# A sixth state pair on GpSimd, a later gated sum and earlier probabilities in a fused Perceiver kernel

## The chip, the cores and the metric

The kernel runs on one core of one Trainium2 chip. The metric is the device time of one execution in microseconds (us). Five engines work side by side, each through its own list of instructions in order: TensorE (PE), VectorE (DVE), ScalarE (ACT), GpSimd (POOL) and SyncE, which starts the DMAs. They meet only through semaphores: an instruction raises one when it is done, and another engine waits until it has a certain value.

## The reference, cut to what matters

The reference is a Perceiver block on x (128 x 32 tokens of 256 numbers) with a context of 128 x 257 tokens. Six layers follow each other, each adding to x. The kernel computes them in two loops; the change is in the first, which holds three things:

```python
x = x + _L0_xattn_ref(ctx_1024, _layernorm(x), wq, wk, wv)      # softmax attention on the context
x = x + _L0_attn_ref(_layernorm(x), W_in, b_in, W_gate, ...)    # gated selective scan, 16 states
# of _L1_xattn_ref, which is linear attention on the same context, only its key side:
k = relu(ctx @ Wk + bk) + eps; k = k / softplus(scale)
k = k**3 / norm(k**3) * norm(k);  kv = k.T @ v;  ks = k.sum()

def _selective_scan(x, delta, A_log, B_mat, C_mat, D_vec):      # inside _L0_attn_ref
    A = -jnp.exp(A_log); c0 = C_mat[0]
    def step(h, inp):
        x_t, d_t = inp
        h = h * jnp.exp(A * d_t[..., None]) + (x_t * d_t)[..., None] * B_mat
        return (h, h @ c0)
    ...
    return y + x * D_vec
```

The 16 states of a channel don't mix: each is a scan of its own over time, and y is a weighted sum of the 16 results. The result is `gate * (y + x * D) @ W_out.T + b_out`.

## The kernel before, in words

**Tiling.** The 128 sequences are cut into 32 groups of four (128 rows of tokens), and four groups make a chunk. The 512 inner channels of the scan are four blocks of 128 channels; one block of one chunk (a 128 x 512 tile) is one scan job, so there are 32 jobs.

**Steps.** The first loop has 37 steps, G = 0 to 36, and software-pipelines four stages (`stages(G)`): A, group G: attention and the first three and a half parts of its keys; C, group G-1: the end of its keys, its Gram products with the context, its key sums; J, scan job G-4; Z, the end of scan job G-5. Steps 5 to 31 have all four stages. Every fourth step from G = 8 on (g == 0) also has the output projection of an earlier chunk ("output step"), and every step with g == 3 up to G = 27 the query projection of the next chunk ("query step"); the others are called plain.

**A scan job.** TensorE projects hT to `delta`, `x` and `gate`, all three through one PSUM bank, so each must be drained before the next is made. ScalarE drains delta (L769), x to `dx` (L787) and gate with a tanh (L811). VectorE makes `u` = x * delta in PSUM (L991). Then for each of eight pairs q of states: ScalarE makes two decays exp(-A delta) into `abuf[q % 2]` (`act_decay`, L696); VectorE runs two scans (`dve_scan`, L943). A buffer of decays is free again when the scan that read it is done, so decay q waits for scan q-2. The results of a pair are added up in one of two ways. Pairs 0, 6 and 7 (BY_PE) go to `gL`, and TensorE multiplies them with diagonal matrices into the bank `ps_y` (`pe_states`, L570). Pairs 1 to 5 (BY_POOL) are weighted in place by ScalarE (`act_weigh`, L705) and added up in `yac` by GpSimd (`pool_add`, L868 for pair 1 with dx, L871 for the others). At the end VectorE makes the gated sum: ps_y + yac[0], + yac[1], times (1 + gate), three instructions (L1010, L1012, L1014) into `yg`, which the output projection reads.

**Keys and attention.** For each of the four sequences b of a group TensorE makes keys (`pe_keys`, L509 and L512), VectorE drains them (`dve_keys`, L952), ScalarE squares them (L718), GpSimd cubes them (`pool_cube`, L861), ScalarE sums the squares of the cubes (L725), GpSimd makes the ratio of norms for two sequences (`pool_ratio`, L851 and L855), ScalarE normalises (L736), TensorE makes the Gram product (`pe_gram`, L524) and ScalarE drains it (L744). The attention: scores (L500), maximum (L969, L974), probabilities (L780), their transposes (L627, L628), a copy (L1001), the product with the context (L643), `o_sb` (L1020), its transposes (L654), the copy `oT` (L1029), the projection (L666), and the layer norm (L834).

**Order.** Nothing is planned at run time. The order on each engine is what `pe_step`, `act_step`, `pool_step` and `dve_step` write down by hand for a step; the semaphores only hold an instruction back.

## Time and profile before

| | us |
|---|---|
| median of 3 executions | 2247.94 (2247.15 to 2249.84) |
| the profiled execution | 2246.96 |
| its span, first to last instruction | 2245.1 |
| busy: TensorE / VectorE / ScalarE / GpSimd | 1864.1 / 1592.2 / 1475.6 / 1207.8 |
| granted TensorE clock, mean | 0.917 |

The page gives these. The 40 slices of the page show TensorE at 80 to 90% busy until about 1290 us of the span and a dip around 1350 to 1450 us, where the first loop runs out (its last scan jobs have no keys beside them) and the second begins. Two more kinds of view are used below: the instructions of one engine in order of time (start, duration, what it is, and in brackets how long the engine had been idle before it and who released it), and the busy time of all engines between two given times.

### The profile page before, as it was taken

Reading aid. Unit: us, or ns where it says so; the run is one execution under the profiler, and the core shown is the slowest. Engines: PE = TensorE matmul, PEld = TensorE weight load, DVE = VectorE, ACT = ScalarE, POOL = GpSimd, SP = SyncE. Lnnn points to the kernel's source line nnn. Section 1 sums busy time; section 2 is a strip of 40 time slices with the busy share of each in tenths; the row PEclk is TensorE's granted clock in tenths of the full one; section 3 lists DMA queues with packets and bytes.
Section 4 is the critical chain, followed back from the end, with each engine's and each line's share of the span. In section 5 each row is a group of like instructions: output and inputs, shape, how many; then the busy total and the mean of one; then the engine's idle time right before and its main releaser. Section 6 shows DMA issues by size and latency. Waiting matters only on the chain. (4 is left out here: it accounts for less than half of the span.)

```text
span 2245.1 us, 41621 instructions
## 1 busy us (share of the span) xinstructions
PE 1864.1 (83%) x14355; PEld 1256.0 (56%) x14355; DVE 1592.2 (71%) x2945; ACT 1475.6 (66%) x3431; POOL 1207.8 (54%) x1300
## 2 busy tenths in 40 slices
PE   4898988988988898899899774378989898888964
PEld 2655555555555555555555432356666666676743
DVE  3348777767867867867858787457788878878763
ACT  2558877777868868867868776124666666656654
POOL 1435555545546545545545633156777767767751
PEclk8999999999999999999999997678889999989876
DMA  7321112112211211111111110100000000000000
GB/s 187 111 90 60 62 55 67 60 54 67 66 56 59 78 59 62 60 61 60 59 52 60 38 47 5 54 7 9 13 12 12 12 12 12 12 12 12 10 8 10
DMA packets 48370, 103.20 MB, mean 46 GB/s; under 512 B 6384, under 2 KB 25072, under 8 KB 43376
## 3 DMA queue, kind: packets, MB, share of 16 engines
q1 hardware_dynamic: 48240, 101.57, 14.4%
q8 instruction: 69, 1.13, 0.2%
q14 instruction: 61, 0.50, 0.1%
HBM read 93.03 MB, written 8.52 MB: 45 GB/s over the span
## 5 line engine op out<-in xcount | busy, mean ns | idle before, releaser
L861 POOL TENSOR_TENSOR kcube<-kcube,ksq 128x512 f32<-128x512 f32 x128 | 178.0, 1391 | 487.2 <-ACT ksq L718 487.2
L696 ACT ACTIVATE abuf<-delta,cols 128x496 f32<-128x496 f32 x512 | 337.6, 699 | 30.5 <-DVE gP L943 19.0
L871 POOL TENSOR_TENSOR yac<-yac,gP 128x1024 f32<-128x1024 f32 x128 | 301.7, 2357 | 11.4 <-ACT gP L705 10.3
L943 DVE TENSOR_TENSOR_SCAN gP<-abuf,ps_s 128x512 f32<-128x512 f32 x256 | 293.3, 1196 | 0.6 <-POOL yac L871 0.6
L943 DVE TENSOR_TENSOR_SCAN gL<-abuf,ps_s 128x512 f32<-128x512 f32 x192 | 223.2, 1206 | 57.7 <-ACT abuf L696 57.6
L583 PE MATMUL ps_kv<-hT,w_pT 128*128 128x512 f32 x384 | 194.0, 630 | 75.0 <-ACT delta L769 72.5
L512 PE MATMUL ps_kv<-w_k,cT 128*128 128x256 f32 x1024 | 256.1, 393 | 0.0
L524 PE MATMUL ps_kv<-kcube,cx 128*128 128x256 f32 x1024 | 246.8, 385 | 9.4 <-ACT kcube L736 8.6
L524 PEld LDWEIGHTS ps_kv<-kcube,cx 128*128 128x128 f32 x1024 | 192.7, 192 | 62.5 <-ACT kcube L736 20.3
L512 PEld LDWEIGHTS ps_kv<-w_k,cT 128*128 128x128 f32 x1024 | 184.7, 190 | 49.4 <-issue 29.4
L570 PE MATMUL ps_t<-gL,diag 128*128 128x512 f32 x384 | 184.7, 605 | 15.4 <-DVE gL L943 13.1
L705 ACT ACTIVATE gP<-gP,cols 128x512 f32<-128x512 f32 x256 | 169.1, 709 | 0.0
L583 PEld LDWEIGHTS ps_kv<-hT,w_pT 128*128 128x128 f32 x384 | 72.8, 198 | 158.9 <-ACT delta L769 99.7
L851 POOL TENSOR_TENSOR rat<-s,roots 128x8 f32<-128x8 f32 x64 | 105.8, 1654 | 79.6 <-ACT junk L725 79.6
L952 DVE TENSOR_TENSOR kcube<-ps_kv,epi 128x512 f32<-128x512 f32 x128 | 86.5, 676 | 80.1 <-PE ps_kv L512 80.1
L725 ACT ACTIVATE junk<-kcube 128x256 bf16<-128x256 f32 x256 | 103.3, 406 | 52.0 <-POOL kcube L861 52.0
L736 ACT ACTIVATE kcube<-kcube,rk 128x256 f32<-128x256 f32 x256 | 108.6, 495 | 28.3 <-POOL rk L855 28.3
L570 PEld LDWEIGHTS ps_t<-gL,diag 128*128 128x128 f32 x384 | 71.5, 193 | 91.5 <-issue 68.8
L1462 PE MATMUL ps_t<-pjT,gT 128*128 128x256 f32 x512 | 117.5, 383 | 0.0
L1591 POOL TENSOR_TENSOR kTm<-kTe,mask 128x1024 f32<-128x1024 f32 x32 | 92.4, 2888 | 45.9 <-ACT kTe L1501 45.9
L744 ACT ACTIVATE Gs<-ps_kv 128x512 f32<-128x512 f32 x128 | 74.5, 582 | 63.1 <-PE ps_kv L524 62.9
L718 ACT ACTIVATE ksq<-kcube 128x256 f32<-128x256 f32 x256 | 102.9, 405 | 8.4 <-DVE kcube L952 8.4
(312 smaller groups left out, 4279.8 us busy)
## 6 DMA issues: line engine op xcount, KB each, us to landing
cT<-in_h_ctxT SPq DMA_DIRECT2D x32, 1028.0 KB, 4.9
cx<-in_ctx SPq DMA_DIRECT2D x32, 1024.0 KB, 5.3
xT<-in_h_xT SPq DMA_DIRECT2D x8, 512.0 KB, 3.9
xcur<-in_x SPq DMA_DIRECT2D x32, 128.0 KB, 2.0
x_mid<-xb SPq DMA_DIRECT2D x16, 256.0 KB, 2.2
x_c<-x_mid SPq DMA_DIRECT2D x32, 128.0 KB, 2.0
out<-y SPq DMA_DIRECT2D x32, 128.0 KB, 1.7
kv_all<-vleft SPq DMA_DIRECT2D x8, 256.0 KB, 11.1
```

The source lines that it names most:

```text
L512: last = pe.matmul(bank[:, j * D:(j + 1) * D], cT[G % 2][:, b, dc, j * P:(j + 1) * P], w_k[:, dc, :], start=False, stop=(dc == DC - 1), sk ...
L524: last = pe.matmul(ps_g[:, dc * D:(dc + 1) * D], cx[G % 2][:, b, j, dc * P:(dc + 1) * P], kcube[N % RING][:, j, :], start=(j == 0), stop=( ...
L570: last = pe.matmul(ps_y[:, :], diag[:, J % CB, 2 * k + i, :], pe_home(J, q)[:, i, :], start=(k == 0 and i == 0), stop=(k == NPE - 1 and i ...
L583: last = pe.matmul(ps_p, w_pT[:, dc, r * P:(r + 1) * P], hT[s % 2][:, dc, :], start=(dc == 0), stop=(dc == DC - 1))
L696: act.activation(abuf[q % 2][:, i, :].rearrange("p (b t) -> p b t", t=T)[:, :, 1:T], delta[J % 2][:, :].rearrange("p (b t) -> p b t", t=T) ...
L705: last = act.activation(t[:, i, :], t[:, i, :], ACT.Copy, scale=w_st[:, J % CB, 2 * q + i:2 * q + i + 1])
L736: last = act.activation(t[:, j, :], t[:, j, :], ACT.Copy, scale=rk[k % 2][:, 2 * i + j:2 * i + j + 1])
L851: pool.tensor_tensor(rat[p][:, :], s26[p][:, :], roots[:, :], ALU.pow).then_inc(S["rat_ready"], 1)
L861: pool.tensor_tensor(t[:, :, :], t[:, :, :], ksq[:, :, :], ALU.mult).then_inc(S["k3_ready"], 1)
L871: pool.tensor_tensor(yac[:, :, :], yac[:, :, :], pool_home(q)[:, :, :], ALU.add).then_inc(S["pacc_done"], 1)
L943: dve.tensor_tensor_scan(dst[:, i, :], abuf[q % 2][:, i, :], ps_u[:, :], 0.0, ALU.mult, ALU.add).then_inc(S["scan_done"], 1)
L1462: last = pe.matmul(ps_c1[:, 0:D], gT[:, f, :], W["pjT"][:, f, :], start=(f == 0), stop=(f == FC - 1))
```

## The change: what it does

Pair 6 goes from the TensorE way to the ScalarE and GpSimd way: ScalarE weights it (behind decay 0 of the next job) and GpSimd adds it. TensorE keeps pairs 0 and 7; the state product of pair 0 is issued a step later, between the delta and the x projection. `gate` and `yac` get two buffers each. On VectorE the gated sum moves from ahead of `o_sb` to behind `oT`, ahead of scan 2, and the key-sum addition (L1082) from behind to ahead of scan 5. On ScalarE the probabilities move from behind weighing 5, a Gram drain and the normalising to right behind delta. On GpSimd the additions move ahead by one place: 4 ahead of the ratio, 5 ahead of cube 0, 6 ahead of cube 1, 2 ahead of the rstd1 power, 3 ahead of cube 3. The diff, with one line of context:

```diff
NPAIR = NST // 2
-BY_POOL = (1, 2, 3, 4, 5)
+BY_POOL = (1, 2, 3, 4, 5, 6)
 BY_PE = tuple(q for q in range(NPAIR) if q not in BY_POOL)
...
         dx = sb("dx", [P, TS])
-        gate = sb("gate", [P, TS])
+        gate = [sb(f"gate{i}", [P, TS]) for i in range(2)]
         abuf = [sb(f"abuf{i}", [P, 2, TS]) for i in range(2)]
...
         gP = [sb(f"gP{i}", [P, 2, TS]) for i in range(3)]
-        yac = sb("yac", [P, 2, TS])
+        yac = [sb(f"yac{i}", [P, 2, TS]) for i in range(2)]
         yg = sb("yg", [P, CB, TS])
...
 
+        if Z is not None:
+            pe_states(pe, Z, 0)
         if J is not None:
             pe_project(pe, "x", J)
-        if Z is not None:
-            pe_states(pe, Z, 6)
         if C is not None:
...
             pe_finish(pe, C)
-        if J is not None:
-            pe_states(pe, J, 0)
         if g == 0 and sc >= 2:
...
 
-    def pool_home(q):
+    def pool_home(J, q):
         k = BY_POOL.index(q)
-        return yac if k == 0 else gP[(k - 1) % 3]
+        return yac[J % 2] if k == 0 else gP[(k - 1) % 3]
 
...
 
-        t = pool_home(q)
+        t = pool_home(J, q)
         for i in range(2):
...
             act.activation(delta[J % 2][:, :], ps_p, ACT.Relu, bias=b_dl[:, J % CB:J % CB + 1]).then_inc(S["pj_act"], 1)
+        if A is not None:
+            act.wait_ge(S["negm_ready"], A + 1)
+            if A:
+                act.wait_ge(S["pT_full"], A)
+            act.activation(pr[:, :], ps_s[:, 0:L], ACT.Exp, bias=negm[:, 0:1], scale=rstd0[:, 0:1],
+                           accum_out=rsum[:, 0:1]).then_inc(S["p_ready"], 1)
         if Z is not None:
...
 
-        if A is not None:
-            act.wait_ge(S["negm_ready"], A + 1)
-            if A:
-                act.wait_ge(S["pT_full"], A)
-            act.activation(pr[:, :], ps_s[:, 0:L], ACT.Exp, bias=negm[:, 0:1], scale=rstd0[:, 0:1],
-                           accum_out=rsum[:, 0:1]).then_inc(S["p_ready"], 1)
         if J is not None:
...
             act_decay(act, J, 0)
+        if Z is not None:
+            act_weigh(act, Z, 6)
         if A is not None:
...
             act.wait_ge(S["pj_full"], filled("gate", J))
-            if J:
-                act.wait_ge(S["yg_ready"], J)
-            act.activation(gate[:, :], ps_p, ACT.Tanh, bias=b_gh[:, J % CB:J % CB + 1], scale=0.5).then_inc(S["pj_act"], 1)
+            if J >= 2:
+                act.wait_ge(S["yg_ready"], J - 1)
+            act.activation(gate[J % 2][:, :], ps_p, ACT.Tanh, bias=b_gh[:, J % CB:J % CB + 1], scale=0.5).then_inc(S["pj_act"], 1)
         if A is not None:
...
             pool.wait_ge(S["pj_act"], act_took("x", J))
-            pool.tensor_tensor(yac[:, 0, :], yac[:, 0, :], dx[:, :], ALU.add).then_inc(S["pacc_done"], 1)
+            pool.tensor_tensor(yac[J % 2][:, 0, :], yac[J % 2][:, 0, :], dx[:, :], ALU.add).then_inc(S["pacc_done"], 1)
         else:
             pool.wait_ge(S["pacc_done"], NADD * J + k)
-            pool.tensor_tensor(yac[:, :, :], yac[:, :, :], pool_home(q)[:, :, :], ALU.add).then_inc(S["pacc_done"], 1)
+            pool.tensor_tensor(yac[J % 2][:, :, :], yac[J % 2][:, :, :], pool_home(J, q)[:, :, :], ALU.add).then_inc(S["pacc_done"], 1)
 
...
         g, sc = G % SG, G // SG
+        if Z is not None:
+            pool_add(pool, Z, 4)
         if C is not None:
...
         if Z is not None:
-            pool_add(pool, Z, 4)
+            pool_add(pool, Z, 5)
         if A is not None:
...
         if Z is not None:
-            pool_add(pool, Z, 5)
+            pool_add(pool, Z, 6)
         if A is not None:
...
             pool_cube(pool, A, 2)
+        if J is not None:
+            pool_add(pool, J, 2)
+        if A is not None:
             pool.wait_ge(S["x_var"], A + 1)
...
         if J is not None:
-            pool_add(pool, J, 2)
+            pool_add(pool, J, 3)
         if A is not None:
...
                 pool_rstd0(pool, A + 1)
-        if J is not None:
-            pool_add(pool, J, 3)
-        if A is not None:
             if sc >= 2 and g % 2 == 0:
...
             k = BY_POOL.index(q)
-            dst = pool_home(q)
-            if k == 0 and J:
-                dve.wait_ge(S["y_summed"], J)
+            dst = pool_home(J, q)
+            if k == 0:
+                if J >= 2:
+                    dve.wait_ge(S["y_summed"], J - 1)
             elif k >= 4:
...
 
+        if A is not None:
+            dve.wait_ge(S["pv_full"], A + 1)
+            if A:
+                dve.wait_ge(S["oT_full"], A)
+            dve.tensor_scalar(o_sb[:, :], ps_m[:, 0:D], rinv[:, 0:1], None, ALU.mult).then_inc(S["o_ready"], 1)
+        if J is not None:
+            dve_scan(dve, J, 1)
+
+        if A is not None:
+            dve_keys(dve, A, 2)
+            dve.wait_ge(S["oT_full"], A + 1)
+            if A:
+                dve.wait_ge(S["o_full"], A)
+            dve.tensor_copy(oT[:, :, :], b3(ps_m[:, 0:D], DC)).then_inc(S["oT_ready"], 1)
         if Z is not None:
...
             out = yg[:, Z % CB, :]
-            dve.tensor_tensor(out, ps_y[:, :], yac[:, 0, :], ALU.add).then_inc(S["y_read"], 1)
+            dve.tensor_tensor(out, ps_y[:, :], yac[Z % 2][:, 0, :], ALU.add).then_inc(S["y_read"], 1)
             dve.wait_ge(S["y_read"], Z + 1)
-            dve.tensor_tensor(out, out, yac[:, 1, :], ALU.add).then_inc(S["y_summed"], 1)
+            dve.tensor_tensor(out, out, yac[Z % 2][:, 1, :], ALU.add).then_inc(S["y_summed"], 1)
             dve.wait_ge(S["y_summed"], Z + 1)
-            dve.scalar_tensor_tensor(out=out, in0=gate[:, :], scalar=1.0, in1=out, op0=ALU.add,
+            dve.scalar_tensor_tensor(out=out, in0=gate[Z % 2][:, :], scalar=1.0, in1=out, op0=ALU.add,
                                      op1=ALU.mult).then_inc(S["yg_ready"], 1)
-        if A is not None:
-            dve.wait_ge(S["pv_full"], A + 1)
-            if A:
-                dve.wait_ge(S["oT_full"], A)
-            dve.tensor_scalar(o_sb[:, :], ps_m[:, 0:D], rinv[:, 0:1], None, ALU.mult).then_inc(S["o_ready"], 1)
-        if J is not None:
-            dve_scan(dve, J, 1)
-
-        if A is not None:
-            dve_keys(dve, A, 2)
-            dve.wait_ge(S["oT_full"], A + 1)
-            if A:
-                dve.wait_ge(S["o_full"], A)
-            dve.tensor_copy(oT[:, :, :], b3(ps_m[:, 0:D], DC)).then_inc(S["oT_ready"], 1)
         if J is not None:
...
                                      op1=ALU.mult).then_inc(S["nbias_ready"], 1)
+        if C is not None:
+            dve.wait_ge(S["kst_full"], C + 1)
+            sums = ps_m[:, 0:D].rearrange("p (c b k) -> p b c k", c=DC, b=GB)[:, :, :, 0]
+            ks = ks_all[:, C * GB:(C + 1) * GB, :]
+            dve.tensor_tensor(ks, ks, sums, ALU.add).then_inc(S["ks_added"], 1)
         if J is not None:
...
             kvn = kvt[:, :, :, :].rearrange("p b c e -> p (b c) e")
-            dve.wait_ge(S["kst_full"], C + 1)
-            sums = ps_m[:, 0:D].rearrange("p (c b k) -> p b c k", c=DC, b=GB)[:, :, :, 0]
-            ks = ks_all[:, C * GB:(C + 1) * GB, :]
-            dve.tensor_tensor(ks, ks, sums, ALU.add).then_inc(S["ks_added"], 1)
             dve.wait_ge(S["kv_half"], C + 1)
...
```

## Rows read from the trace of the kernel before

**Rows 1.** The page's costliest groups: busy us, mean ns of one, idle before.
```profile
L871 POOL TENSOR_TENSOR yac<-yac,gP 128x1024 f32<-128x1024 f32 x128 | 301.7, 2357 | 11.4 <-ACT gP L705 10.3
...
L570 PE MATMUL ps_t<-gL,diag 128*128 128x512 f32 x384 | 184.7, 605 | 15.4 <-DVE gL L943 13.1
L705 ACT ACTIVATE gP<-gP,cols 128x512 f32<-128x512 f32 x256 | 169.1, 709 | 0.0
```

**Rows 2.** Busy time by stretch, gate to gate: step 4, plain, output, query.
```profile
166.73:204.08 37.35, 33.20 (x188) 20.75 (x187) 28.24 (x43) 30.99 (x77) 21.50 (x16) 1.00 0.19 61
859.26:896.69 37.43, 33.30 (x188) 20.78 (x187) 29.59 (x45) 31.09 (x77) 21.53 (x16) 1.00 0.18 58
813.20:859.26 46.06, 41.84 (x220) 27.95 (x219) 29.72 (x46) 31.09 (x77) 21.54 (x16) 0.96 0.19 62
1098.99:1140.86 41.87, 36.74 (x196) 22.35 (x195) 30.61 (x46) 32.16 (x80) 21.51 (x16) 1.00 0.17 54
```

**Rows 3.** ScalarE in order of time, plain step: start us, us; idle in brackets.
```profile
859.26 0.69 ACT L811 ACTIVATE gate<-ps_kv,cols 128x512 f32<-128x512 f32 x1 [2.10 <-PE ps_kv L583]
...
864.88 0.71 ACT L696 ACTIVATE abuf<-delta,cols 128x496 f32<-128x496 f32 x1 [0.40 <-DVE gP L943]
...
876.43 0.19 ACT L718 ACTIVATION_READ_ACCUMULATOR ksq<-kcube 128x1 f32 x1
...
883.48 1.71 ACT L736 ACTIVATE kcube<-kcube,rk 128x256 f32<-128x256 f32 x4 [0.83 <-POOL rk L855]
...
896.69 0.69 ACT L811 ACTIVATE gate<-ps_kv,cols 128x512 f32<-128x512 f32 x1 [2.10 <-PE ps_kv L583]
```

**Rows 4.** TensorE in order of time, same step.
```profile
881.00 1.99 PE L583 MATMUL ps_kv<-hT,w_pT 128*128 128x512 f32 x4 [2.19 <-ACT delta L769]
...
884.53 1.90 PE L524 MATMUL ps_kv<-kcube,cx 128*128 128x256 f32 x8
```

**Rows 5.** GpSimd in order of time, same step.
```profile
856.76 1.75 POOL L861 TENSOR_TENSOR kcube<-kcube,ksq 128x512 f32<-128x512 f32 x1 [0.88 <-ACT ksq L718]
...
876.70 1.27 POOL L861 TENSOR_TENSOR kcube<-kcube,ksq 128x512 f32<-128x512 f32 x1 [4.51 <-ACT ksq L718]
...
883.24 0.20 POOL L855 TENSOR_TENSOR rk<-rat 128x4 f32<-128x4 f32 x1
```

**Rows 6.** VectorE in order of time, same step.
```profile
855.97 0.69 DVE L1010 TENSOR_TENSOR yg<-ps_t,yac 128x512 f32<-128x512 f32 x1 [1.66 <-issue]
...
857.42 1.64 DVE L1014 SCALAR_TENSOR_TENSOR yg<-gate,yg 128x512 f32<-128x512 f32 x1
858.98 0.47 DVE L1020 TENSOR_SCALAR o_sb<-ps_m,rinv 128x256 f32<-128x256 f32 x1
...
862.53 4.53 DVE L943 TENSOR_TENSOR_SCAN gP<-abuf,ps_s 128x512 f32<-128x512 f32 x4
```

**Rows 7.** VectorE, then ScalarE, in order of time, step 4 (no gated sum).
```profile
165.01 0.48 DVE L1020 TENSOR_SCALAR o_sb<-ps_m,rinv 128x256 f32<-128x256 f32 x1 [3.04 <-PE ps_m L645]
...
168.97 0.69 DVE L952 TENSOR_TENSOR kcube<-ps_kv,epi 128x512 f32<-128x512 f32 x1 [1.24 <-PE ps_kv L512]
...
169.91 4.54 DVE L943 TENSOR_TENSOR_SCAN gP<-abuf,ps_s 128x512 f32<-128x512 f32 x4
...
169.31 1.33 ACT L705 ACTIVATE yac<-yac,cols 128x512 f32<-128x512 f32 x2
```

**Rows 8.** Line L1014: durations in ns, least, median and greatest.
```profile
L1014 DVE SCALAR_TENSOR_TENSOR yg<-gate,yg x32: 691/1637/1654, 202.2 to 1392.5; 128x512 f32<-128x512 f32 x32
```

**Rows 9.** TensorE in order of time, output, slow x and query steps.
```profile
818.38 3.62 PE L593 MATMUL ps_kv<-w_oT,yg 128*128 128x256 f32 x16
...
825.50 5.38 PE L593 MATMUL ps_kv<-w_oT,yg 128*128 128x256 f32 x16 [2.64 <-DVE xb L959]
...
1044.35 3.59 PE L583 MATMUL ps_kv<-hT,w_pT 128*128 128x512 f32 x4 [2.30 <-ACT delta L769]
...
1128.70 1.89 PE L524 MATMUL ps_kv<-kcube,cx 128*128 128x256 f32 x8
```

More of the change, by code:

```diff
@@ L769, in act_step @@
             act.activation(delta[J % 2][:, :], ps_p, ACT.Relu, bias=b_dl[:, J % CB:J % CB + 1]).then_inc(S["pj_act"], 1)
-        if Z is not None:
-            act_weigh(act, Z, 5)
-        if C is not None:
-            act_gram(act, C, 1)
-            act_normalise(act, C, 1)
         if A is not None:
@@ L781, in act_step @@
                            accum_out=rsum[:, 0:1]).then_inc(S["p_ready"], 1)
+        if Z is not None:
+            act_weigh(act, Z, 5)
+        if C is not None:
+            act_gram(act, C, 1)
+            act_normalise(act, C, 1)
         if J is not None:
@@ L875, in pool_step @@
         g, sc = G % SG, G // SG
+        if Z is not None:
+            pool_add(pool, Z, 4)
         if C is not None:
@@ L1001, in dve_step @@
             dve.tensor_copy(pT[:, :], ps_m[:, 0:3 * P]).then_inc(S["pT_ready"], 1)
-        if Z is not None:
-            dve.wait_ge(S["y_full"], NPE * (Z + 1))
-            dve.wait_ge(S["pacc_done"], NADD * (Z + 1))
-            dve.wait_ge(S["pj_act"], act_took("gate", Z))
-            if Z >= CB:
-                dve.wait_ge(S["pj_full"], filled("wo", 2 * (Z // CB - 1) + 1))
-            out = yg[:, Z % CB, :]
-            dve.tensor_tensor(out, ps_y[:, :], yac[:, 0, :], ALU.add).then_inc(S["y_read"], 1)
-            dve.wait_ge(S["y_read"], Z + 1)
-            dve.tensor_tensor(out, out, yac[:, 1, :], ALU.add).then_inc(S["y_summed"], 1)
-            dve.wait_ge(S["y_summed"], Z + 1)
-            dve.scalar_tensor_tensor(out=out, in0=gate[:, :], scalar=1.0, in1=out, op0=ALU.add,
-                                     op1=ALU.mult).then_inc(S["yg_ready"], 1)
         if A is not None:
@@ L1029, in dve_step @@
             dve.tensor_copy(oT[:, :, :], b3(ps_m[:, 0:D], DC)).then_inc(S["oT_ready"], 1)
+        if Z is not None:
+            dve.wait_ge(S["y_full"], NPE * (Z + 1))
+            dve.wait_ge(S["pacc_done"], NADD * (Z + 1))
+            dve.wait_ge(S["pj_act"], act_took("gate", Z))
+            if Z >= CB:
+                dve.wait_ge(S["pj_full"], filled("wo", 2 * (Z // CB - 1) + 1))
+            out = yg[:, Z % CB, :]
+            dve.tensor_tensor(out, ps_y[:, :], yac[Z % 2][:, 0, :], ALU.add).then_inc(S["y_read"], 1)
+            dve.wait_ge(S["y_read"], Z + 1)
+            dve.tensor_tensor(out, out, yac[Z % 2][:, 1, :], ALU.add).then_inc(S["y_summed"], 1)
+            dve.wait_ge(S["y_summed"], Z + 1)
+            dve.scalar_tensor_tensor(out=out, in0=gate[Z % 2][:, :], scalar=1.0, in1=out, op0=ALU.add,
+                                     op1=ALU.mult).then_inc(S["yg_ready"], 1)
         if J is not None:
@@ L1073, in dve_step @@
                                      op1=ALU.mult).then_inc(S["nbias_ready"], 1)
+        if C is not None:
+            dve.wait_ge(S["kst_full"], C + 1)
+            sums = ps_m[:, 0:D].rearrange("p (c b k) -> p b c k", c=DC, b=GB)[:, :, :, 0]
+            ks = ks_all[:, C * GB:(C + 1) * GB, :]
+            dve.tensor_tensor(ks, ks, sums, ALU.add).then_inc(S["ks_added"], 1)
         if J is not None:
```

## The prediction, as it was put on record

> **What bounds the kernel now.** The change touches only the first of the two big loops, up to about 1400 us of the span, so I read that loop and leave the rest as it is. I read the page's groups first, for prices [rows 1]; then the busy times between two starts of the gate activation (L811), which come once a step and give a step's length [rows 2]; then one plain step, 859.26 to 896.69 us, on each engine in order of time [rows 3 to 6]; then step 4, which has no gated sum and so shows part of the new order [rows 7]. A plain step takes 37.43 us, of which TensorE is busy 33.30, ScalarE 31.09, VectorE 29.59 and GpSimd 21.53 [rows 2]: none is full, so a ring of waits sets the step and must be found. I measure all times from the start of the gate activation ("gate").
>
> The ring, forwards from gate at 859.26:
> (a) ScalarE makes the decays of pair 4 only when scans of pair 2 have let go of the buffer. Its second half starts at 864.88, 5.62 us behind gate, released by VectorE [rows 3]. VectorE came late because its gated sum started only at 855.97, behind a wait of 1.66, and scans 1 and 2 stand behind it; scan 2 starts at 862.53 [rows 6].
> (b) From 864.88 ScalarE has no wait until its last key square, whose accumulator is out at 876.43 + 0.19 = 876.62: 11.74 us.
> (c) GpSimd waited 4.51 us for that square and then works through cube 3, rstd, an addition, the x copy and the ratio: from 876.70 to the second ratio instruction at 883.24 [rows 5]. ScalarE starts normalising keys at 883.48, after 0.83 us of waiting: 6.86 us from the square's end.
> (d) TensorE's third Gram product needs the first normalised keys; it starts at 884.53, 1.05 us later [rows 4].
> (e) From there TensorE has no gap to the end of the gate projection, which releases gate at 896.69 after 2.10 us of idle ScalarE [rows 3]: 12.16 us.
> 5.62 + 11.74 + 6.86 + 1.05 + 12.16 = 37.43, the measured step. Everything else has slack.
>
> **The change, part by part.**
>
> Pair 6 leaves TensorE. Four matmul instructions a step go, of 605 ns modelled each [rows 1], some 1.7 us of TensorE's pitch. They stood between the x projection, started at 881.00, and the third Gram product at 884.53 [rows 4]. But that product also needs the normalised keys: two of the four ScalarE pieces from 883.48, so about 884.4 (the four take 1.71). What goes from (d) is therefore only about 0.08 us; then keys are late there instead of TensorE. The rest becomes a TensorE gap of about 1.6 us. I take -0.08; bounds 0 and -0.13.
>
> State products of pair 0, moved between the delta and x projections, fill the wait of 2.19 us for ScalarE's delta [rows 4]. What they left, behind the Gram finish, has slack. In a plain step this is worth 0.
>
> Pair 6 on ScalarE: two weighings of 0.709 [rows 1], 1.22 in pitch, behind decay 0. They fall between normalising and gate, where ScalarE has 2.10 us of idle time. The probabilities (one short activation) move ahead of the normalising, where ScalarE waited 0.83 [rows 3], so it still starts on GpSimd's word. VectorE's u product and dx come earlier, but no term of the ring contains them. Sum 0; were the cover gone, weighing 6 would cost 1.22.
>
> Pair 6 on GpSimd: one addition of 2.36 [rows 1]. In the stretch (c) the additions only change places: addition 3 goes ahead of cube 3 into the 4.51 us gap, addition 4 comes between the x copy and the ratio. Same instructions, same 6.86. Addition 6 and the earlier addition 5 fill the gaps around cubes 0 and 1. Addition 2 is now ahead of rstd1, on which the layer norm (L834) waits; as I count it, it is ready about 0.4 us in time. Sum 0; if it isn't, some tenths.
>
> The key-sum addition ahead of scan 5 removes a wait of TensorE, one of those in its 37.43 - 33.30 = 4.1 us of gaps [rows 2], but it is ahead of delta, outside the ring: 0. So are the waits that the second gate and the second accumulator remove: 0.
>
> The gated sum, behind the output copy and ahead of scan 2. This decides. Three instructions: 855.97 to 858.98 [rows 6], 3.0 us. They leave a place where they delayed scan 1 and enter one where they delay scan 2. What scan 2 is worth there, step 4 shows, where no gated sum stands at all: VectorE waits for the attention product, copies at 165.01, scans pair 1, then waits 1.24 us for keys 2, at 168.97, because TensorE makes keys 2 only behind the gate projection; scan 2 starts at 169.91 [rows 7], which is gate (166.73) + 3.18. So even without the gated sum scan 2 cannot start before gate + 3.18 (+3.27 in the plain step [rows 3, 6]). With it in front: 3.18 + 3.0 = 6.2. ScalarE's second decay of pair 4 starts 2.35 us behind scan 2 (864.88 against 862.53 [rows 3, 6]), so (a) becomes 8.54 instead of 5.62: +2.92. ScalarE stands meanwhile from about gate + 3.8 (weighing 1 at +2.58 [rows 7]), behind it weighings, squares, decays, and all of (b). Gone are its two small waits, which cost (a) nothing more.
>
> How long the sum takes there: its third instruction takes 1.64 in the median but 0.69 at least [rows 8]. In the plain step a cube on GpSimd, at 856.76, takes 1.75 [rows 5] and overlaps the sum (its third instruction: 857.42, 1.64 [rows 6]); without such company it would be 0.95 less. In the new place dx's addition follows weighing 1, at about gate + 3.98, when the sum's second instruction has just begun (+3.9): the same meeting as now. I take 3.0; bounds 2.05 and 3.0. The Trainium skill says in "SBUF — State Buffer", section Terms, that of VectorE and GpSimd the loser of their shared ports blocks fully; by that page 3.0 stands if the two meet and 2.05 if not, as in the rows.
>
> Plain steps: 5.62 + 2.92 = 8.54; 8.54 + 11.74 + 6.86 + 0.97 + 12.16 = 40.27 us, +2.84. There are 15 among the 27 steps (5 to 31) that have all four stages: +42.6.
>
> Query steps (6): 41.87 now [rows 2]. The same 2.92 comes into ScalarE's row of work. At their end TensorE is late itself: delta, x, pair 6 and then the third Gram product at 1128.70 [rows 9]. Without pair 6 that is 1.7 earlier, with pair 0 now ahead of x 0.9 later, and the normalised keys, then late, take 0.3: -0.5. +2.4 each, +14.4.
>
> Output steps (6): 46.06 now [rows 2]. TensorE's first output product, now at 818.38 (gate + 5.18), needs this step's gated sum and moves to + 6.3. It then stands behind a gap of about 2.8 us instead of none. Now the second one stands behind a gap of 2.64 and takes 5.38 where the first takes 3.62 [rows 9]. I take 5.38 for both by that row: 1.1 + 1.8 = 2.9, with latencies 3.0; bound below 1.2 (full clock). +18.
>
> In three of the plain steps the x projection took 3.59 behind a gap of 2.30 [rows 9], and the step was 1.6 longer. In the new order x has 1.6 us of slack, so 3 x 1.6 = 4.8 go. The start, the drain of the loop and the second loop: 0.
>
> Sum: 42.6 + 14.4 + 18 - 4.8 = +70. The profiled execution took 2246.96 us (span 2245.1), 0.98 under the median of 2247.94, so 2317 by it, 2318 by the median: 2317.
>
> **Rivals.**
> 1. The gated sum meets no GpSimd work: 2.05 instead of 3.0, 27 x 0.95 = 26 less: 2291. For it: the least is 0.69 [rows 8], and the meeting is timed to 0.1 us. Against: the median.
> 2. TensorE's clock. TensorE will have more gaps: about 3.4 us ahead of the first Gram product (normalising comes 2.9 later), 1.8 ahead of x, 1.6 to 1.8 ahead of the third Gram product, on the ring. If what follows the last gap runs at half clock, as x did for 3.59 instead of 1.99 [rows 4, 9], each step loses up to 1.7: 27 x 1.7 = 46: 2363. Against: 2.19 us gaps mostly leave the clock at 1.00 now [rows 2], and each gap on the ring is shorter. "TensorE: Matmul & The Clock Gate" of the Trainium skill, Part 1, says the throttled clock is the default and activity releases it; by that page more gaps mean more of this rival.
> 3. The other side: scan 2 is not what ScalarE waits for, and (a) falls to what its own instructions need: 2.58 to weighing 1 [rows 7], 1.22 for it and 0.6 for a decay, 4.4. The step is then 1.2 shorter, and 27 x 1.2 = 32 go: 2215. Its place is decay 4, and it decides if scan 2's first half is done before gate + 3.8. For it: VectorE has only 30 us of work in a step. Against: step 4 puts scan 2's start at + 3.18 with no gated sum ahead.
> 4. TensorE, the busiest engine, is the bound after all: 1.7 us x 27 = 46 less, 2201. Against: its gaps of 4.1 us a step [rows 2].
>
> **How the numbers follow.** Forecast 52%, rival 1 12%, rival 2 (whole or in part) 22%, rival 3 7%, rival 4 2%; the other 5% are offsetting errors that end at no change or slightly off it. The range takes rival 1 whole and rival 2 mostly: 2284 to 2354. 0.2% is 4.5 us, about what a measurement here can tell. Faster 0.09, same 0.04, slower 0.87.
>
> **What would show it.** Plain steps of 40.3 us between gate starts; scan 2 (L943 gP) at gate + 6.2; ScalarE's decay of pair 4 with waits of about 3.5 and 0.4 for VectorE; GpSimd's cube-3-to-ratio stretch unchanged at 6.8; a TensorE gap ahead of the third Gram product; VectorE's wait for the probabilities (L983) gone without any gain in the step. Wrong it would be if ScalarE reaches decay 4 without a wait, or if the step is shorter than 37.4.

## The result, and the profile after

| | median of the runs | range | span of the profiled execution |
|---|---|---|---|
| before | 2247.55 us | 2246.49 to 2249.84 | 2245.1 |
| after | 2374.55 us | 2374.42 to 2375.07 | 2373.3 |

The change makes the kernel slower: ratio 1.0564 [1.0548, 1.0581], +127 us where +70 was forecast. The direction and the main step were right; the size was not, and the time lies 21 us above the top of the range (2354).

Where the 128.2 us of span came in, as sums between gate starts of the two traces (steps as in [rows 2]):

| stretch | before | after | difference | forecast |
|---|---|---|---|---|
| up to the first gate | 166.7 | 167.1 | +0.4 | 0 |
| step 4 | 37.35 | 39.22 | +1.9 | 0 |
| 15 plain steps | 566.0 | 651.0 | +85.0 | +42.6 |
| 6 query steps | 252.8 | 282.9 | +30.1 | +14.4 |
| 6 output steps | 276.4 | 285.1 | +8.7 | +18 |
| the rest, behind step 31 | | | +2 | 0 |

(The forecast's -4.8 for slow x projections belongs to the plain steps as well.) The stretches of after that answer to [rows 2], gate to gate: two plain steps, a query step, an output step. Columns: window, its length, busy time of TensorE, its weight loads, VectorE, ScalarE and GpSimd (in brackets their instructions), the granted clock, the DMA share, GB/s.

```profile
791.99:834.37 42.38, 35.12 (x184) 21.49 (x183) 31.54 (x45) 32.20 (x79) 23.78 (x17) 0.92 0.17 52
972.40:1016.66 44.26, 36.56 (x184) 22.27 (x183) 31.65 (x45) 32.33 (x80) 23.77 (x17) 0.88 0.15 51
834.37:880.89 46.52, 36.92 (x192) 21.92 (x191) 31.82 (x45) 33.40 (x81) 23.84 (x17) 0.96 0.19 61
880.89:928.21 47.32, 40.33 (x216) 27.28 (x215) 30.85 (x47) 32.21 (x79) 23.76 (x17) 0.96 0.18 58
```

TensorE has four matmuls fewer in a plain step than before, those of pair 6 (184 against 188), and yet is busy for 35.12 instead of 33.30 us, at a granted clock of 0.92 instead of 1.00. The shortest plain steps take 42.09, the longest 44.50; before they took 37.4, three of them 39.0.

The plain step 791.99 to 834.37 in order of time, first ScalarE (start, us; idle before it in brackets):

```profile
791.99 0.69 ACT L811 ACTIVATE gate<-ps_kv,cols 128x512 f32<-128x512 f32 x1 [2.67 <-PE ps_kv L583]
...
799.41 0.71 ACT L694 ACTIVATE abuf<-delta,cols 128x496 f32<-128x496 f32 x1 [3.52 <-DVE gP L946]
...
800.52 0.71 ACT L694 ACTIVATE abuf<-delta,cols 128x496 f32<-128x496 f32 x1 [0.40 <-DVE gP L946]
...
810.18 0.60 ACT L834 ACTIVATE lnh<-xcur,nbias,rstd 128x256 f32<-128x256 f32 x1 [1.63 <-DVE nbias L1075]
...
813.82 0.18 ACT L716 ACTIVATION_READ_ACCUMULATOR ksq<-kcube 128x1 f32 x1
...
820.86 1.71 ACT L734 ACTIVATE kcube<-kcube,rk 128x256 f32<-128x256 f32 x4 [0.28 <-POOL rk L855]
```

The second half of pair 4's decay starts at gate + 8.53 (forecast 8.54), behind waits of 3.52 and 0.40 (forecast "about 3.5 and 0.4"). That is the main step, to a hundredth. Further down stands what the forecast did not have: the layer norm waits 1.63 us for `nbias`, and so the last key square is out at 814.00, 13.48 behind the decay, where [rows 3] gave 11.74. The next two fences are VectorE and then GpSimd of the same step.

```profile
798.17 4.54 DVE L946 TENSOR_TENSOR_SCAN gP<-abuf,ps_s 128x512 f32<-128x512 f32 x4
...
807.85 2.29 DVE L1075 SCALAR_TENSOR_TENSOR nbias<-mv,rstd 128x1 f32<-128x1 f32 x1 [0.26 <-POOL rstd L897]
```

```profile
795.97 1.73 POOL L868 TENSOR_TENSOR yac<-yac,dx 128x512 f32<-128x512 f32 x1 [0.42 <-ACT yac L703]
...
803.70 1.27 POOL L861 TENSOR_TENSOR kcube<-kcube,ksq 128x512 f32<-128x512 f32 x1 [6.00 <-ACT ksq L716]
804.93 2.37 POOL L871 TENSOR_TENSOR yac<-yac,gP 128x1024 f32<-128x1024 f32 x1
807.26 0.56 POOL L897 TENSOR_TENSOR rstd<-ve,nhalf 128x1 f32<-128x1 f32 x1
807.79 2.35 POOL L871 TENSOR_TENSOR yac<-yac,gP 128x1024 f32<-128x1024 f32 x1
814.09 1.26 POOL L861 TENSOR_TENSOR kcube<-kcube,ksq 128x512 f32<-128x512 f32 x1 [3.95 <-ACT ksq L716]
```

`nbias` is one number a partition. It takes 0.15 us in every step of before, and here 2.29. It is released by rstd at 807.82; at 807.79 GpSimd, which has nothing to wait for, has begun addition 3 (L871), and that ends at 810.14. `nbias` ends at 807.85 + 2.29 = 810.14 too. Of the 32 steps 22 have this 2.29; steps 0 to 3 and the six output steps have 0.15.

TensorE of the same step, and two rows of the 44.26 us step:

```profile
802.08 3.61 PE L524 MATMUL ps_kv<-kcube,cx 128*128 128x256 f32 x8 [3.36 <-ACT kcube L734]
...
810.84 0.44 PE L608 MATMUL ps_m<-ident,lnh 128*128 128x128 f32 x2 [1.68 <-ACT lnh L834]
...
818.38 3.16 PE L583 MATMUL ps_kv<-hT,w_pT 128*128 128x512 f32 x4 [1.94 <-ACT delta L767]
821.82 2.29 PE L524 MATMUL ps_kv<-kcube,cx 128*128 128x256 f32 x8 [0.28 <-ACT kcube L734]
...
998.79 2.68 PE L583 MATMUL ps_kv<-hT,w_pT 128*128 128x512 f32 x4 [1.94 <-ACT delta L767]
1002.23 3.78 PE L524 MATMUL ps_kv<-kcube,cx 128*128 128x256 f32 x8 [0.76 <-ACT kcube L734]
```

The large products behind the gaps take up to twice what they took before: x 3.16 for 1.99 (2.68 in the longer step), the third Gram product 2.29 and in the longer step 3.78 for 1.90 [rows 4]; the first Gram product takes 3.61 here and 1.99 in the query step that follows. 3.78 is 1.99 times 1.9: by its length it ran at the lower of TensorE's two levels (1.2 GHz) for nearly all of it, and the granted clock of that step is 0.88. The third Gram product lies on the ring. The ring of this step, by the forecast's parts: 8.53 + 13.48 + 6.86 + 0.96 + 12.55 = 42.38. (c) and (d) are as forecast.

### The profile page after: what moved, and what is told of

Read it like the earlier page. It is cut to its first block and busy times, and to the rows that moved or that the text cites. A ratio compares the mean times of both kernels' runs of the same rounds, so it can differ in the third digit from the quotient of the medians.

```text
span 2373.3 us, 41452 instructions
## 1 busy us (share of the span) xinstructions
PE 1888.5 (80%) x14196; PEld 1269.2 (53%) x14227; DVE 1636.5 (69%) x2937; ACT 1511.6 (64%) x3495; POOL 1280.9 (54%) x1332
## 3 DMA queue, kind: packets, MB, share of 16 engines
q1 hardware_dynamic: 48240, 101.57, 13.5%
## 5 line engine op out<-in xcount | busy, mean ns | idle before, releaser
L861 POOL TENSOR_TENSOR kcube<-kcube,ksq 128x512 f32<-128x512 f32 x128 | 165.0, 1289 | 504.1 <-ACT ksq L716 504.1
L871 POOL TENSOR_TENSOR yac<-yac,gP 128x1024 f32<-128x1024 f32 x160 | 376.6, 2354 | 60.0 <-ACT gP L703 58.6
L524 PE MATMUL ps_kv<-kcube,cx 128*128 128x256 f32 x1024 | 293.8, 438 | 106.6 <-ACT kcube L734 105.3
L946 DVE TENSOR_TENSOR_SCAN gP<-abuf,ps_s 128x512 f32<-128x512 f32 x320 | 368.1, 1199 | 0.5 <-POOL yac L871 0.5
L524 PEld LDWEIGHTS ps_kv<-kcube,cx 128*128 128x128 f32 x1024 | 214.6, 217 | 191.6 <-ACT kcube L734 145.4
L583 PE MATMUL ps_kv<-hT,w_pT 128*128 128x512 f32 x384 | 200.7, 648 | 51.7 <-ACT delta L767 41.6
L703 ACT ACTIVATE gP<-gP,cols 128x512 f32<-128x512 f32 x320 | 211.4, 709 | 0.0
L946 DVE TENSOR_TENSOR_SCAN gL<-abuf,ps_s 128x512 f32<-128x512 f32 x128 | 149.0, 1206 | 73.0 <-ACT abuf L694 72.3
L570 PE MATMUL ps_t<-gL,diag 128*128 128x512 f32 x256 | 126.6, 618 | 17.1 <-DVE gL L946 13.2
L1010 DVE TENSOR_SCALAR o_sb<-ps_m,rinv 128x256 f32<-128x256 f32 x32 | 15.5, 484 | 143.1 <-PE ps_m L645 143.1
```

Of the source, the lines that this page charges most:

```text
L524: last = pe.matmul(ps_g[:, dc * D:(dc + 1) * D], cx[G % 2][:, b, j, dc * P:(dc + 1) * P], kcube[N % RING][:, j, :], start=(j == 0), stop=( ...
L570: last = pe.matmul(ps_y[:, :], diag[:, J % CB, 2 * k + i, :], pe_home(J, q)[:, i, :], start=(k == 0 and i == 0), stop=(k == NPE - 1 and i ...
L583: last = pe.matmul(ps_p, w_pT[:, dc, r * P:(r + 1) * P], hT[s % 2][:, dc, :], start=(dc == 0), stop=(dc == DC - 1))
L703: last = act.activation(t[:, i, :], t[:, i, :], ACT.Copy, scale=w_st[:, J % CB, 2 * q + i:2 * q + i + 1])
L861: pool.tensor_tensor(t[:, :, :], t[:, :, :], ksq[:, :, :], ALU.mult).then_inc(S["k3_ready"], 1)
L871: pool.tensor_tensor(yac[J % 2][:, :, :], yac[J % 2][:, :, :], pool_home(J, q)[:, :, :], ALU.add).then_inc(S["pacc_done"], 1)
```

## The experiments

Unless said otherwise an experiment is an edit of the kernel after; times are medians with the ratio to the kernel before on the same chip (2246.95 to 2249.02). Plain steps are read gate to gate. e3, e8, e9, e10 and e12 hold filler matmuls more, whose product nobody reads.

**e1: the gated sum back in its old place**

```
-        if Z is not None: <gated sum, behind the copy to oT>
+        if Z is not None: <gated sum, ahead of the copy to o_sb>
```

> The changed kernel with only the gated sum put back ahead of o_sb; all else stays. If its new place behind the output copy delays scan 2 and with it the fourth decay (my theory), the second decay of pair 4 comes back from gate + 8.5 to about gate + 5.5, ScalarE's 3.5 us wait there goes, and plain steps are some 3 us shorter: about 39.4 us where the clock is full, the whole 2375 - 27 x 2.9 = about 2297, less if TensorE's clock recovers with it (down to 2260). The layer norm's wait of 1.6 us for nbias stays. Rival (pair 6 on GpSimd and ScalarE costs the time itself): 2360 to 2375.

2297.42 us, 1.0212 [1.0134, 1.0289], from two executions that lie 14 us apart (2290.21 and 2304.63). Some 77 of the 127 us (the interval is 17 us wide to either side) go with the place of three instructions. Its plain steps take 39.07 at the least, six of them 41.2 to 41.5: in the one shown the 3.52 us wait ahead of the decay has shrunk to 0.52, the layer norm's wait of 1.63 stays. ScalarE in it:

```profile
420.15 0.71 ACT L694 ACTIVATE abuf<-delta,cols 128x496 f32<-128x496 f32 x1 [0.52 <-DVE gP L946]
...
430.92 0.60 ACT L834 ACTIVATE lnh<-xcur,nbias,rstd 128x256 f32<-128x256 f32 x1 [1.63 <-DVE nbias L1075]
```

**e2: rstd1 ahead of addition 2**

```
-        if J is not None:
-            pool_add(pool, J, 2)
         if A is not None:
             ...                       # rstd1 (L897)
+        if J is not None:
+            pool_add(pool, J, 2)
```

> The changed kernel with only the rstd1 power put back ahead of addition 2 on GpSimd. nbias on VectorE takes 2.3 us in the changed kernel (0.15 before) and the layer norm waits 1.63 us for it, on the ring. Theory: rstd1 ends while VectorE waits and addition 3 follows at once, so nbias is shut out from the ports until it is over; with rstd1 early nbias takes 0.15, and 28 steps lose 1.6 us: about 2330. Rival (the layer norm's wait is covered by something else on the ring): within 10 us of 2375.

2329.24 us, 1.0353 [1.0323, 1.0383]: 45 us less than after, from moving one instruction of 0.56 us ahead of one of 2.37. A plain step of it: the window, then ScalarE, VectorE and TensorE.

```profile
1120.71:1161.06 40.35, 33.59 (x184) 20.67 (x183) 29.78 (x45) 32.09 (x79) 23.84 (x17) 0.96 0.18 58
```

```profile
1120.71 0.69 ACT L811 ACTIVATE gate<-ps_kv,cols 128x512 f32<-128x512 f32 x1 [2.67 <-PE ps_kv L583]
...
1128.14 0.71 ACT L694 ACTIVATE abuf<-delta,cols 128x496 f32<-128x496 f32 x1 [3.52 <-DVE gP L946]
...
1129.25 0.71 ACT L694 ACTIVATE abuf<-delta,cols 128x496 f32<-128x496 f32 x1 [0.40 <-DVE gP L946]
```

```profile
1136.62 0.15 DVE L1075 SCALAR_TENSOR_TENSOR nbias<-mv,rstd 128x1 f32<-128x1 f32 x1
```

```profile
1145.37 1.98 PE L583 MATMUL ps_kv<-hT,w_pT 128*128 128x512 f32 x4 [1.94 <-ACT delta L767]
...
1148.81 1.99 PE L524 MATMUL ps_kv<-kcube,cx 128*128 128x256 f32 x8 [1.46 <-ACT kcube L734]
```

This is the plain step that was forecast: 40.35 (forecast 40.27), decay at gate + 8.54, third Gram product at gate + 28.10 (28.11), a gap of 1.46 ahead of it (1.6). `nbias` takes 0.15 and the layer norm has no wait. Thirteen of the fifteen plain steps take 40.3 to 40.8, two 42.5; the gated sum costs 15 x (40.34 - 37.4) = 44 us in them.

**e4: only the late gated sum, put into the kernel before** (with the two gates and the two accumulators that it needs; pair 6 stays on TensorE)

```
-        if Z is not None: <gated sum, ahead of the copy to o_sb>
+        if Z is not None: <gated sum, behind the copy to oT>
```

> The kernel before with only the two buffers for gate and accumulator and the gated sum behind the output copy; pair 6 stays on TensorE. Theory: scan 2 starts at gate + 6.2, plain steps take 40.3 us, the whole about 2247.5 + 27 x 2.9 - 5 = about 2320. Rival (the place of the sum is harmless without pair 6): 2248.

2335.44 us, 1.0381 [1.0351, 1.0411]. The plain steps take 40.35, every other one 42.0, and the decay waits 3.52 and 0.4: the term belongs to the gated sum alone, without pair 6 and without the moved additions. Two plain steps that follow each other:

```profile
558.31:598.67 40.36, 33.73 (x188) 20.57 (x187) 29.69 (x45) 30.99 (x77) 21.50 (x16) 1.00 0.18 57
598.67:640.70 42.03, 35.40 (x188) 21.31 (x187) 29.79 (x45) 31.09 (x77) 21.48 (x16) 0.96 0.17 54
```

TensorE is idle for 6.63 us in both, and the clock is 1.00 in one and 0.96 in the other. The total is 15 over what was expected, and 31.9 us came in the query steps (most 47.9 instead of 41.9). Their second query projection starts at gate + 17.63 instead of + 14.71, so 6 x 2.92 = 17.5 is the gated sum's delay; the other 14 are slow products: that projection takes 3.75 in five of the six, and the scores and keys behind it up to 1.94 and 3.18, for 1.95, 1.08 and 1.99 in the short query steps of before.

**e5: addition 3 behind cube 3 (shown), and addition 4 behind the ratio**, rstd1 left where it is, behind addition 2. If rstd1 is merely late, nothing changes; if it is addition 3 that shuts VectorE out, `nbias` is short again.

```
             pool.tensor_tensor(rstd1[:, :], ve1[:, :], nhalf[:, 0:1], ALU.pow).then_inc(S["x_rstd"], 1)
-        if J is not None:
-            pool_add(pool, J, 3)
         if A is not None:
             ...                       # cube 3
+        if J is not None:
+            pool_add(pool, J, 3)
```

> The changed kernel with rstd1 left behind addition 2, but with additions 3 and 4 back behind cube 3 and behind the ratio, so that GpSimd has nothing to do right behind rstd1. It tells two reasons for the late layer norm apart. Theory (VectorE's nbias is shut out by addition 3): nbias takes 0.15 to 0.3 us instead of 2.3, the layer norm waits 0 to 0.2 us, 28 steps lose 1.6: about 2330. Rival (rstd1 itself comes too late behind addition 2): the layer norm still waits 1 us or more, and the whole stays within 15 us of 2375.

2402.66 us, 1.0691 [1.067, 1.0713], 73 above what was expected and 28 above after. The cause is told apart all the same. VectorE and GpSimd of one of its plain steps:

```profile
826.40 0.16 DVE L1076 SCALAR_TENSOR_TENSOR nbias<-mv,rstd 128x1 f32<-128x1 f32 x1 [0.26 <-POOL rstd L897]
...
835.03 2.33 DVE L947 TENSOR_TENSOR_SCAN gP<-abuf,ps_s 128x512 f32<-128x512 f32 x2 [4.85 <-POOL yac L871]
```

```profile
825.82 0.55 POOL L897 TENSOR_TENSOR rstd<-ve,nhalf 128x1 f32<-128x1 f32 x1
830.90 1.26 POOL L861 TENSOR_TENSOR kcube<-kcube,ksq 128x512 f32<-128x512 f32 x1 [4.53 <-ACT ksq L716]
...
832.65 2.35 POOL L871 TENSOR_TENSOR yac<-yac,gP 128x1024 f32<-128x1024 f32 x1
```

`nbias` waits the same 0.26 for the same rstd as in after, but with GpSimd idle behind it takes 0.16, and the layer norm has no wait. So rstd1's lateness costs nothing; what costs is the operation that follows it on GpSimd. The new loss stands one row lower: pair 6 is scanned into the buffer that pair 3 used, and waits 4.85 us for addition 3. A step of 44.4. I had moved the addition without asking who waits for its buffer.

**e6: both undone** (e1 and e2 together; pair 6, the earlier probabilities, additions and state products stay)

> The changed kernel with both undone: gated sum ahead of o_sb and rstd1 ahead of addition 2. Pair 6 stays on GpSimd. If the two costs are separate and all there is, plain steps are 37.4 us and the whole is 2297 - 45 = 2252, the time of the kernel before within 10 us. Rival (pair 6 costs something of its own): 2265 or more. Rival (the emptier TensorE or the earlier probabilities bring a gain of their own): 2240 or less.

2239.01 us, 0.9958 [0.9946, 0.9969], 13 less than expected. The plain steps add up: e1 took 49.7 us off them, e2 40.4, both together 89.9. That the whole gained 136 and not 77 + 45 lies within e1's interval. All 15 plain steps take 37.3 to 37.8 and none 39.0, worth 5 us as forecast for x; the output steps are 15.7 shorter in sum. Pair 6 on GpSimd, the earlier probabilities, the second buffers and the other moved additions, taken together, are therefore not part of the loss; with the sum and rstd1 in their old places they are a gain of 0.4%. What each is worth by itself no run shows.

**e3 and e8: filler matmuls in TensorE's gaps** (ahead of x, behind x, and ahead of the first Gram product; e3 in every step, e8 only in g = 1 and 2)

```
+            pe.matmul(ps_k[bank][:, 0:n], ident[:, :], w_pT[:, 0, 0:n], start=True, stop=True, skip_group_check=True)
```

> The changed kernel with extra matmuls that nobody reads, into key banks that are free just then: 3.0 us of them ahead of the first Gram product, 1.7 ahead of x, 1.3 behind x. Theory: the third Gram product takes 2.3 to 3.8 us in the changed kernel (1.9 before) only because TensorE's clock is at its lower level behind the gaps; with the gaps filled it takes 1.9, plain steps of 42.1 to 44.4 all fall to about 42.0, and the whole to about 2335 to 2345. Rival (the product is slow because its operands or its neighbours are): it stays slow, and the whole is 2375 or more.

> The changed kernel with the filler matmuls only in steps with g = 1 or 2, where TensorE has the gaps. In the run with fillers everywhere those steps took 42.1 or 42.9, against 42.1 to 44.4 without, and the output and query steps lost 3 to 4 us each, because there TensorE has no time for them. Theory (clock): plain steps 42.1 to 42.9, output and query steps as in the changed kernel, the whole 10 to 18 us less: 2357 to 2365. Rival: plain steps stay up to 44.4 or the others grow: 2375 or more.

e3: 2413.32 us, 1.0727 [1.0696, 1.0758]; e8: 2369.6, 1.0544 [1.0523, 1.0565]. A plain and an output step of e3, and the third Gram product of another plain step:

```profile
1186.38:1229.38 43.00, 39.42 (x200) 24.10 (x199) 31.57 (x45) 32.21 (x79) 23.95 (x17) 0.96 0.16 53
1092.84:1144.29 51.45, 45.93 (x232) 30.48 (x231) 30.85 (x47) 32.34 (x79) 23.81 (x17) 0.97 0.17 55
```

```profile
1174.13 1.99 PE L524 MATMUL ps_kv<-kcube,cx 128*128 128x256 f32 x8 [0.17 <-ACT kcube L745]
```

With the gaps filled the third Gram product takes 1.99, and the plain steps 42.1 to 43.0, the last 43.7: of the 19.6 us that they had over 15 x 42.09 in after, 7.6 are left, so most of that was the clock. But an output step, in which TensorE was already busy for 40.33 of 47.32 us, now takes 51.45. e3's loss is there and in the query steps: 21.9 us more in each of the two kinds, against 12.0 less in the plain steps.

e8 ends 5 us under after, with intervals that overlap, and above the 2357 to 2365 that was expected. Its plain steps lose 11.7 us, about as in e3. But the delta and x projections of a step stand ahead of its gate, so the filler of the steps with g = 1 falls, gate to gate, into the output steps: they take 7.2 us more in sum. The query steps, without filler, take 5.1 more.

**e7: e6, with the ratio ahead of addition 4 and weighing 5 at the end of the step**

```
-        if Z is not None:
-            pool_add(pool, Z, 4)
         if C is not None:
             ...                       # the x copy and the ratio
+        if Z is not None:
+            pool_add(pool, Z, 4)
```

> As the last one, and the ratio ahead of addition 4 on GpSimd, and weighing 5 at the end of the step on ScalarE, where it stands idle 1.4 us for cube 3. If the stretch from the last key square to the normalising (6.86 us) is on the ring, it falls to what ScalarE needs itself, about 5.3; plain steps 35.8, the whole about 27 x 1.6 = 43 less, 2210, which would beat both kernels. Rival (TensorE's x projection or the weighings take its place): within 10 us of the last kernel.

2238.71 us, 0.9957 [0.9941, 0.9974], where 2210 was expected. Step 4 and two of the plain steps take 35.8 to 36.1, as worked out, but the others 37.3 to 37.6 (the last 38.5). First a short one, then one of these, and its x and third Gram product:

```profile
403.13:438.92 35.79, 32.14 (x184) 19.77 (x183) 29.55 (x44) 32.10 (x80) 23.96 (x17) 1.00 0.19 62
560.93:598.25 37.32, 33.67 (x184) 20.68 (x183) 31.37 (x45) 32.18 (x79) 23.91 (x17) 0.95 0.19 59
```

```profile
582.59 3.11 PE L583 MATMUL ps_kv<-hT,w_pT 128*128 128x512 f32 x4 [1.95 <-ACT delta L767]
585.49 2.51 PE L524 MATMUL ps_kv<-kcube,cx 128*128 128x256 f32 x8
```

TensorE is idle for 3.65 us in both, with a clock of 1.00 in the short and 0.95 in the long one. The 1.6 us saved on GpSimd are given back by TensorE's clock.

**e9, e10: e7 with two filler matmuls ahead of x (g = 1, 2); then three more ahead of the second output product and three ahead of the second query projection**

```
+            if A is not None and g in (1, 2):
+                pe_filler(pe, 1, GB * A, 2)
             pe_project(pe, "x", J)
```

> The kernel with sum and rstd1 back, ratio first and weighing 5 early (2238.7), and in steps with g = 1 or 2 two extra matmuls that nobody reads ahead of the x projection, where TensorE waits 1.95 us. Its plain steps took 35.8 us in four cases and 37.3 to 37.6 in the others, with x at 2.7 to 3.2 instead of 2.0. Theory (the clock eats what the shorter ring brings): all plain steps fall to about 35.9, 14 x 1.3 = 18 less, about 2220. Rival (the ring has another wait there): within 5 us of 2238.

> As the last one, with three more such matmuls in the gap of 2.65 us ahead of the second output product (which takes 5.37 instead of 3.62) and in the gap of 3.0 us ahead of the second query projection. Theory (clock): 1.7 us less in each of 6 output steps and up to 1.5 in query steps, 10 to 18 us less than the last one, about 2205. Rival (the fillers end late and delay what follows, as they did in e3): the same or more than the last one.

2233.01 us, 0.993 [0.9911, 0.9948], and 2218.93, 0.9862 [0.9835, 0.9889]. Both in the direction, and 13 to 14 short of the size. Gate to gate e9's filler falls into the first plain step behind an output step, which goes from 37.6 to 35.8, and into the output step itself, where x had no gap: 44.2 instead of 42.8, 8.6 us in sum, and about what the plain steps gain (9.0). Six of the plain steps that hold none stay at 37.6. With the filler of e10 the second output product takes 3.69 instead of 5.38 and the output steps 42.5, and four of those six plain steps fall to 36.1 to 36.3 with no filler in them.

**e11: after, with three decay buffers.** It takes away what makes ScalarE wait and leaves the gated sum late.

```
-        abuf = [sb(f"abuf{i}", [P, 2, TS]) for i in range(2)]
+        abuf = [sb(f"abuf{i}", [P, 2, TS]) for i in range(3)]
```

> The changed kernel with three buffers of decays instead of two, so that decay 4 no longer waits for scan 2 but for scan 1. All else stays, the gated sum too. Theory: ScalarE's waits of 3.52 and 0.40 us at decay 4 go; then VectorE's own row sets the layer norm, because the gated sum's 3.0 us stand ahead of scan 2: scan 2 at gate + 6.2, nbias 9.7 later, the layer norm at gate + 16.1 instead of + 18.2. Plain steps 40.2, the whole about 2310 to 2325. Rival (the wait at decay 4 hid nothing, or is not what binds): 2365 to 2375.

2299.55 us, 1.0234 [1.0213, 1.0254], below the expectation: 75 us less than after. The decays' idle time in the whole kernel, after and then e11:

```profile
L694 ACT ACTIVATE abuf<-delta,cols 128x496 f32<-128x496 f32 x512 | 335.3, 698 | 112.1 <-DVE gP L946 112.1
```

```profile
L694 ACT ACTIVATE abuf<-delta,cols 128x496 f32<-128x496 f32 x512 | 331.4, 697 | 0.0
```

It was the buffer, then, through which the late sum reached the decays. But the step is 39.6 and not 37.4: without that way the late sum delays the layer norm through VectorE's own row. ScalarE, then VectorE:

```profile
1288.29 0.60 ACT L834 ACTIVATE lnh<-xcur,nbias,rstd 128x256 f32<-128x256 f32 x1 [2.73 <-DVE nbias L1075]
```

```profile
1288.11 0.14 DVE L1075 SCALAR_TENSOR_TENSOR nbias<-mv,rstd 128x1 f32<-128x1 f32 x1
```

The layer norm starts at gate + 15.7 (16.1 expected), against 18.2 in after, 16.5 in e2 and 13.5 before. `nbias` comes late there, but it is short (0.14 to 0.16 in all 32 steps): VectorE has been busy without a pause and reaches it only when addition 3 is over. So the 75 us hold two gains. 45 of them are the shut-out's, if e2's price holds here; some 30 are the late sum's, less than half of what e1 gave back. The sum still makes the step 2.2 us longer than before.

**e12: e10 with three decay buffers**

> e10 with three buffers of decays. The waits of 0.52 and 0.40 us at decay 4 go as well: 0.6 to 0.9 us less in each of 27 steps, about 2185 to 2190. Rival (VectorE's row to the layer norm, or TensorE, is next at once): within 5 us of e10.

2196.42 us, 0.9787 [0.9759, 0.9815]: 2.1% under before, the best of all, and 6 above the 2185 to 2190 that was expected. A plain step:

```profile
1010.04:1045.37 35.33, 31.93 (x184) 19.86 (x183) 30.40 (x46) 31.99 (x80) 24.00 (x17) 1.00 0.19 62
```

Of 15 plain steps 13 take 35.0 to 35.7, the one shown at a clock of 1.00. ScalarE is busy for 31.99 and TensorE for 31.93 of the 35.33 us, so little is left for a ring of waits to give back; which of the two would bind next no run shows.

## Why the prediction was right in kind and short in size

**The gated sum: right.** Forecast 8.54 for (a), +2.84 a plain step, +42.6 in all. Measured 8.53, and with `nbias` mended (e2) +2.94, 44 us. e4 makes it alone, e1 takes it away, and e11, without the buffer that hands it on, makes its way shorter by some 0.8 us of 2.9: then VectorE's own row carries it to the layer norm. The three instructions took 3.0 us (the last of them 1.64), so rival 1 (2.05) is false. Rival 3 is false with the 3.52 us wait, rival 4 because the plain steps grew while TensorE had four matmuls fewer.

**rstd1 behind addition 2, costed at 0: the step that failed.** The forecast put it: "Addition 2 is now ahead of rstd1, on which the layer norm (L834) waits; ... ready about 0.4 us in time. Sum 0; if it isn't, some tenths." The timing nearly held: `nbias` waits 0.26 us for rstd. What was missing is that addition 3 now stands directly behind rstd1 on GpSimd, and begins 0.06 us before `nbias` does: VectorE's 0.15 us operation is then shut out until the 2.35 us addition ends. Price: a wait of 1.63 us in (b), 22 steps. By experiment (e2) it is 45 us: about 40 in the plain steps, of which 15 x (42.09 - 40.34) = 26 is the wait itself and the rest, 14, clock that went with it; 8 in the query steps; 2 in step 4; less some 2 in the output steps and some 3 ahead of the first gate. The forecast had cited the very rule. "SBUF — State Buffer" of the Trainium skill, section Terms, says that the loser of the ports shared by VectorE and GpSimd blocks fully; I applied it to the gated sum, where the meeting was nothing new, and not to the smallest operation on the ring, where it was. The trace agrees with it: 0.15 against 2.29, nothing between, and both end at 810.14. e5 shows that it takes the addition: the same wait for rstd with GpSimd idle behind it leaves `nbias` at 0.16.

**The clock (rival 2): true beside the forecast, not instead of it.** Plain steps lose 19.6 us over 15 x 42.09, where before lost 5.0 over 15 x 37.4: +15, of the 26 that the rival's 1.7 a step gives for 15 steps. e3 and e8 show it. I had weighed it as an alternative at 22%; it should have stood in the sum with a part of its price. And with `nbias` mended most of it goes (e2: 5.5), though the gap ahead of x is 1.94 in both: that gap alone does not decide it.

"TensorE: Matmul & The Clock Gate" of the Trainium skill, Part 1, has it that the throttled clock is the default and activity releases it. The trace agrees in part. Among steps shown of three kernels the clock is higher where TensorE is idle for less: 0.92 and 0.88 in the two steps of after (7.3 and 7.7 us idle), 0.96 in the step of e2 (6.8), 1.00 in that of e12 (3.4). But between steps of one kernel it does not go by the sum of the gaps: 6.63 us idle went with 1.00 and with 0.96 in e4, 3.65 with 1.00 and with 0.95 in e7, and the 42.09 us steps of after, with 8.2 to 8.4 us idle, had 0.96. What in a step, or in the one ahead of it, decides between the two is left open.

**Output steps: too dear** (+18 forecast, +8.7 measured). The first product moved to gate + 6.31 and took 5.41, as forecast. The second was put at 5.38 as well. The output step of after:

```profile
887.20 5.41 PE L593 MATMUL ps_kv<-w_oT,yg 128*128 128x256 f32 x16 [2.88 <-DVE yg L1031]
...
896.12 3.69 PE L593 MATMUL ps_kv<-w_oT,yg 128*128 128x256 f32 x16 [2.65 <-DVE xb L962]
```

Against [rows 9], 3.62 and then 5.38, the slow one has only changed places: behind the same gap of 2.65 the second now runs at full clock. +1.1 of delay stays, and +1.8 did not come. That is no rule of the order: in e2, with the same order, the second takes 5.38 in two of the six. The error of 9 us offsets part of the others; without it the total would have been further off.

**Query steps: too cheap** (+14.4 forecast, +30.1 measured). The second query projection, of before and then of after:

```profile
1113.71 1.95 PE L486 MATMUL ps_kv<-xT,m_qk 128*128 128x512 f32 x4 [2.61 <-issue]
```

```profile
853.74 3.37 PE L486 MATMUL ps_kv<-xT,m_qk 128*128 128x512 f32 x4 [4.73 <-issue]
```

It starts at gate + 14.7 in every query step of before and at + 19.37 in every one of after: 4.66 later, as much as the layer norm (2.92 from the gated sum, 1.74 with `nbias`). The shortest query step of after takes 46.12, with this projection at full clock: 4.25 over 41.87, so the forecast's own +2.4 is about right and 1.74 x 6 = 10 us are the term that it lacked. The other 5 are the clock: the other five query steps take 46.5 to 48.2, with this projection at up to 3.39 or with a slow product near it. (e2 gives back 8 in these steps and not 10, because slow products cost some 2 us more in its six.)

**Pair 6, the probabilities, the second buffers, costed at 0: right, as far as their sum goes.** e6 keeps them and is 0.4% under before; VectorE's wait for the probabilities, 3.8 us in most steps of before, is gone in after (2.0 stay in the output steps), and no part of the ring became shorter by it. The slow x steps went in e6, as said, but in after other slow products took their place.

## What to carry to other kernels

What a moved operation costs is the time of what now stands behind it, on its own engine and on every engine that shares something with it. When an operation on GpSimd is put behind another, ask not only whether its result is in time, but also what GpSimd starts in the moment of release: a long two-input addition there makes a 0.15 us VectorE operation 2.29 us long, and moving one line gives back 45 us. A rival that can come true together with the forecast belongs in the sum with part of its price. A third buffer, where one engine waits for another to let go, gave back 75 us (e11); but it did not replace the order: 45 of these are the price of the shut-out, which went because `nbias` came later, and the late sum found another way to the ring.
